# Key projections moved from ahead of the batch loop into its first steps, with bulk loads issued by ScalarE, in a decoder-layer kernel

## The reference, cut to what matters

```python
qkv = jnp.einsum('bsd,de->bse', x, qkv_weights).reshape(-1, 3 * D)      # D = 256, H = 16 heads of Dh = 16
q, k, v = the three thirds of qkv, each reshaped to (-1, S, H, Dh) and transposed to heads
a = q @ k / 4, masked to the lower triangle;  a = softmax(a);  heads = a @ v
x = layernorm(x + heads)
x = layernorm(x + retention-like cross attention of x with ctx, using Wq, Wk, Wv)
x = layernorm(x + shared SwiGLU + top 2 of 8 routed SwiGLU experts)
```

## Time and profile before

| what | value |
|---|---|
| median of 3 executions | 768.1 us (765.79 to 771.39) |
| the profiled execution | 769.79 us |
| its span, first to last instruction | 768.0 us |
| mean granted TensorE clock | 0.971 of 2.4 GHz |
| busy over the span: PE / DVE / ACT / POOL | 92% / 62% / 53% / 43% |

### The profile page before, as it was taken

How to read it: one execution, slowest core, us unless ns; L and a number is a source line. 1 busy time by engine, 2 the same in 40 slices (tenths; PEclk the granted TensorE clock), 3 DMA queues, 4 the chain that set the end, 5 groups by cost and what they waited for, 6 DMA issues and landing times.

```text
span 768.0 us, 19404 instructions
## 1 busy us (share of the span) xinstructions
PE 702.7 (92%) x5464; PEld 531.7 (69%) x5465; DVE 479.0 (62%) x1536; ACT 409.2 (53%) x1167; POOL 333.8 (43%) x483
## 2 busy tenths in 40 slices
PE   6977899999999999999987649999999999999993
PEld 5866788888888888888875315566666666665453
DVE  3555577888888888888865433444444444438984
ACT  0268688888888888888851102333333333312232
POOL 1002233345555555555565553555555555541111
PEclk9999999999999999999999768999999999999998
DMA  8745562223333332333371543322222222218962
GB/s 296 249 146 155 149 220 75 82 65 101 102 90 90 101 112 77 102 101 98 91 235 53 155 138 117 125 89 83 89 82 89 82 89 82 89 59 319 307 213 82
DMA packets 77032, 97.54 MB, mean 127 GB/s; under 512 B 12320, under 2 KB 63264, under 8 KB 75936
## 3 DMA queue, kind: packets, MB, share of 16 engines
q1 hardware_dynamic: 59920, 68.21, 28.5%
q0 software_dynamic: 6816, 19.00, 6.9%
q10 hardware_dynamic: 10224, 9.42, 4.6%
HBM read 60.02 MB, written 36.56 MB: 126 GB/s over the span
## 4 chain that ended last, share of the span: by engine, by line
PE 69%; issue 13%; DVE 4%; POOL 4%; SPq 4%; DMA 4%; ACT 1%; DVEq 0%; POOLq 0%; ACTq 0%
PE ps L996 16%; PE ps L1007 8%; PE ps L783 6%; PE ps L861 4%; PE ps L771 4%; PE ps L793 4%; PE ps L748 4%; PE ps L864 3%; PE ps L885 3%; PE ps L751 3%; DVE products L1269 3%; PE ps L982 2%; POOL sent L640 2%; PE ps L989 2%; PE ps L922 2%
## 5 line engine op out<-in xcount | busy, mean ns | idle before, releaser
L1085 ACT ACTIVATE prob<-ps,nmax 128x128 f32<-128x128 f32 x512 | 146.4, 377 | 29.1 <-DVE nmax L1259 29.0
L996 PE MATMUL ps<-first_use,xgT 128*128 x284 | 135.6, 600 | 1.5 <-ACT xgT L1190 1.5
L1489 DVE TENSOR_TENSOR hid<-ps,attn_only 128x512 f32<-128x512 f32 x71 | 49.1, 692 | 95.6 <-PE ps L996 94.4
L1190 ACT COPY xgT<-ps 128x256 f32<-128x256 f32 x71 | 26.4, 372 | 137.2 <-PE ps L982 137.2
L1259 DVE TENSOR_REDUCE nmax<-ps 128x4 f32<-128x512 f32 x128 | 82.2, 685 | 19.9 <-PE ps L771 18.5
L677 POOL TENSOR_TENSOR gate_h<-hid,sil 128x256 f32<-128x256 f32 x71 | 50.8, 715 | 96.6 <-DVE result_row L1502 83.0
L1092 ACT COPY pT<-ps 128x512 f32<-128x512 f32 x128 | 76.7, 599 | 18.9 <-PE ps L783 14.7
L783 PE MATMUL ps<-tf,prob 128*128 128x128 f32 x512 | 78.2, 275 | 5.7 <-ACT pT L1092 5.7
L996 PEld LDWEIGHTS ps<-first_use,xgT 128*128 128x128 f32 x284 | 54.3, 192 | 40.5 <-issue 37.0
L640 POOL DMA_INDIRECT sent<-packets,pos x64 | 63.7, 995 | 37.3 <-PE ps L771 22.8
L680 POOL DMA_INDIRECT back<-yg,result_row x71 | 71.5, 1007 | 14.3 <-issue 12.4
(11 more groups left out here) (135 smaller groups left out, 1408.8 us busy)
## 6 DMA issues: line engine op xcount, KB each, us to landing
xg<-sent ACTq DMA_DIRECT2D x68, 129.5 KB, 2.1
first_use<-back SPq DMA_DIRECT2D x8, 1024.0 KB, 7.9
k_dram<-first_use SPq DMA_DIRECT2D x4, 1024.0 KB, 4.4
attn_only<-in_x_turned SPq DMA_DIRECT2D x32, 128.0 KB, 3.0
attn_only<-k_dram SPq DMA_DIRECT2D x256, 16.0 KB
attn_only<-in_x SPq DMA_DIRECT2D x32, 128.0 KB, 2.8
attn_only<-in_ctx SPq DMA_DIRECT2D x32, 128.0 KB, 2.9
first_use<-in_L_ffn_rw SPq DMA_DIRECT2D x8, 512.0 KB, 5.2
```

The lines of the kernel that those rows point to most:

```text
L996: mm = eng.matmul(ps[:, r, :], xgT[:, r, c, :], rw1_sb[:, bass.ds(e * (DC * 2 * FFN) + c * 2 * FFN, 2 * FFN)], start=(c == 0), stop=(c == ...
L1085: ins = eng.activation(prob[:, t % 2, 4 * u + n, :], SCORE[u][:, n * P:(n + 1) * P], ACT.Exp, bias=nmax[:, t % 2, 4 * u + n:4 * u + n + 1])
```

## The change

- Keys: a table `K_BANK` gives each of the 16 quarters its PSUM bank. Quarters 0 to 3 (group 0) run ahead of the loop, 4 to 6 at the head of step 0, ahead of its scores; 7 to 9 in the rest of step 0, 10 to 13 in step 1, 14 and 15 in step 2. DVE's copies are spread to match.
- SP no longer loads groups 1 to 3 nor runs `load_small`. ACT issues them: group 1 ahead of its steps once group 0's last piece is in, group 2 at the head of its step 0, group 3 after the first exponentials of step 0, and `load_small` (8 transfers) between the third and the fourth set of exponentials of step 0. The mask table is loaded early on SP with a semaphore of its own.
- The store of group 0 is split: the rows of batch 0 (128 KB), then the rest. SP's stores of groups 1 to 3 move to the ends of its steps 0, 1 and 2.
- Waits for the tables, cross-attention weights and small weights move to steps 3 and 5; the expert weights begin loading in step 4 in place of 3; POOL's clearing of `sent` moves from step 2 to 4.

```diff
+K_BANK = (4, 5, 6, 7, 4, 5, 7, 4, 5, 7, 5, 7, 5, 7, 6, 7)
@@ SP
-            for g in range(1, NG):
-                eng.dma_start(xTu[g][:, :, :, :, :].rearrange("p u c b i -> p (u c b i)"),
-                              x_blocks[g].rearrange("p u n -> p (u n)")).then_inc(xTu_in[g], 16)
-            eng.dma_start(ident, table_f32[:, 0:P]).then_inc(ident_in, 16)
             for n in (0, 2):
                 eng.dma_start(wqkv_sb[:, :, n * D:(n + 1) * D], wqkv_rows[:, :, n * D:(n + 1) * D]).then_inc(w_in, 16)
+            eng.dma_start(xT[:, 0, :, :], x_turned[0]).then_inc(xT_in[0], 16)
+            eng.dma_start(tb[:, :], table_bf16).then_inc(mask_in, 16)
+            eng.dma_start(xT[:, 1, :, :], x_turned[1]).then_inc(xT_in[1], 16)
+            eng.dma_start(ident, table_f32[:, 0:P]).then_inc(ident_in, 16)
...
             def store_k(g):
                 eng.wait_ge(kk_set, g * 4 + 4)
-                eng.dma_start(k_dram[g * GB:(g + 1) * GB].rearrange("b i g f -> (b i) (g f)"),
-                              kk_of(g)).then_inc(k_stored[min(g, 1)], 16)
-
-            load_small()
+                rows = k_dram[g * GB:(g + 1) * GB].rearrange("b i g f -> (b i) (g f)")
+                if g == 0:
+                    eng.dma_start(rows[0:DH, :], kk_of(g)[0:DH, :]).then_inc(k_stored[0], 16)
+                    eng.dma_start(rows[DH:P, :], kk_of(g)[DH:P, :]).then_inc(k_stored[1], 16)
+                else:
+                    eng.dma_start(rows, kk_of(g)).then_inc(k_stored[2], 16)
+
             store_k(0)
@@ SP step
-                    if t == 0:
-                        eng.wait_ge(k_stored[0], 16)
+                    if t < 2:
+                        eng.wait_ge(k_stored[t], 16)
...
-                if n in (-1, 0, 1):
-                    store_k(n + 2)
-                if n == 3:
-                    eng.wait_ge(k_stored[1], 16 * (NG - 1))
-                if 2 < n <= 2 + NE // 2:
+                if n == 4:
+                    eng.wait_ge(k_stored[2], 16 * (NG - 1))
+                if 3 < n <= 3 + NE // 2:
...
                     eng.dma_start(xn[:, t % 2, :], x[t]).then_inc(xn_in[t % 2], 16)
+                if n in (0, 1, 2):
+                    store_k(n + 1)
@@ POOL step
-                if n == 2:
+                if n == 4:
                     eng.wait_ge(zeros_set, 1)
@@ PE
+            def project_ks(first, end):
+
+                for i in range(first, end):
+                    if i == 0:
+                        eng.wait_ge(wk_in, 16)
+                    if i < 4:
+                        eng.wait_ge(first_in[i], 16)
+                    elif i % 4 == 0:
+                        eng.wait_ge(xTu_in[i // 4], 16)
+                    if K_BANK[i] in K_BANK[:i]:
+                        eng.wait_ge(kk_set, i - K_BANK[:i][::-1].index(K_BANK[i]))
+                    project_k(i // 4, i % 4, K_BANK[i])
+
+            project_ks(0, 4)
             eng.wait_ge(w_in, 32)
-            eng.wait_ge(kk_set, 4 * NG - 5)
-            eng.wait_ge(tables_in, 32)
-            eng.wait_ge(xw_in, 48)
-            eng.wait_ge(small_in, 64)
+            eng.wait_ge(mask_in, 16)
             eng.wait_ge(consts_set, 2)
+            eng.wait_ge(kk_set, 3)
@@ PE step
+                if n == 0:
+                    project_ks(4, 7)
                 if n == 1:
-                    eng.wait_ge(kk_set, 13)
+                    eng.wait_ge(ident_in, 16)
+                    eng.wait_ge(kk_set, 8)
...
                 if n == 2:
-                    eng.wait_ge(kk_set, 4 * NG)
+                    eng.wait_ge(kk_set, 13)
...
                 if live(n):
                     scores(n)
                 if n == 0:
-                    eng.wait_ge(kk_set, 9)
-                    project_k(NG - 1, 0, 4)
+                    project_ks(7, 9)
                 if n == 1:
-                    eng.wait_ge(kk_set, 14)
-                    project_k(NG - 1, 3, 5)
+                    project_ks(10, 11)
+                if n == 2:
+                    eng.wait_ge(q_set, 3)
+                    eng.wait_ge(v_set, 3)
+                    project_ks(14, 15)
...
                 if live(n - 1):
                     turn_probs(n - 1, 1)
+                if n == 1:
+                    project_ks(11, 12)
...
                 if live(n - 1):
                     turn_probs(n - 1, 2)
+                if n == 1:
+                    project_ks(12, 13)
+                if n == 2:
+                    project_ks(15, 16)
...
+                if n == 2:
+                    eng.wait_ge(kk_set, 15)
                 if live(n + 1):
                     project(n + 1)
                 if n == 0:
-                    eng.wait_ge(kk_set, 12)
-                    project_k(NG - 1, 1, 5)
-                    project_k(NG - 1, 2, 7)
+                    project_ks(9, 10)
+                if n == 1:
+                    project_ks(13, 14)
@@ ACT
+            def load_small():
+                eng.dma_start(tf[:, P:], table_f32[:, P:]).then_inc(tables_in, 16)
+                for w, src in ((xwq_sb, xwq), (xwk_sb, xwk), (xwv_sb, xwv)):
+                    eng.dma_start(w[:, :, :], src.rearrange("(c p) n -> p c n", p=P)).then_inc(xw_in, 16)
+                eng.dma_start(gate_w_sb[:, :, :], gate_w.rearrange("(c p) n -> p c n", p=P)).then_inc(small_in, 16)
+                eng.dma_start(gate_b_sb[:, 0:NE], gate_b.rearrange("(o n) -> o n", o=1).broadcast_to([P, NE])).then_inc(small_in, 16)
+                eng.dma_start(sb1_sb[:, :], sb1[0].rearrange("(c p) -> p c", p=P), allow_slow_non_contiguous=True).then_inc(small_in, 16)
+                eng.dma_start(sb2_sb[:, :], sb2.broadcast_to([P, D])).then_inc(small_in, 16)
+
+            eng.wait_ge(first_in[3], 16)
+            load_blocks(1)
@@ ACT step
+                if n == 0:
+                    load_blocks(2)
...
                 if live(n):
                     exps(n, 1)
+                if n == 0:
+                    load_blocks(3)
...
                 if live(n):
                     exps(n, 3)
+                if n == 0:
+                    load_small()
@@ DVE step
+                if n == 0:
+                    out_ks(4, 7)
...
+                if n == 1:
+                    out_ks(9, 10)
+                if n == 2:
+                    out_ks(13, 14)
...
                 if n == 0:
-                    for j, bank in enumerate((4, 5, 7)):
-                        out_k(NG - 1, j, bank)
+                    out_ks(7, 9)
                 if n == 1:
-                    out_k(NG - 1, 3, 5)
+                    out_ks(10, 12)
+                if n == 2:
+                    out_ks(14, 15)
...
+                if n == 2:
+                    out_ks(15, 16)
...
                 if live(n) and live(n + 1):
                     lay_mask(n + 1, 3)
+                if n == 1:
+                    out_ks(12, 13)
```

More of the change, by code:

```diff
@@ L292, in decoder_kernel @@
         kk_set = sem("kk_set")
-        k_stored = [sem("k_stored_first"), sem("k_stored_rest")]
+        k_stored = [sem("k_stored_batch"), sem("k_stored_group"), sem("k_stored_rest")]
+        mask_in = sem("mask_in")
         xT_in = [sem("xT_in0"), sem("xT_in1")]
@@ L467, in step @@
                 t = n + 2
-                if live(t):
+                if live(t) and t > 1:
                     after(eng, qv_made, t - 1)
@@ L835, in step @@
             def step(n):
+                if n == 0:
+                    project_ks(4, 7)
                 if n == 1:
-                    eng.wait_ge(kk_set, 13)
+                    eng.wait_ge(ident_in, 16)
+                    eng.wait_ge(kk_set, 8)
+                if n == 3:
+                    eng.wait_ge(tables_in, 16)
+                    eng.wait_ge(xw_in, 48)
+                if n == 5:
+                    eng.wait_ge(small_in, 64)
                 if live(n - 1):
@@ L957, in step @@
                     eng.wait_ge(x1_set, t + 1)
+                    if n == 2:
+                        eng.wait_ge(kk_set, 4 * NG)
                     after(eng, gc_set, n - 4)
@@ L1241, in _, with out_ks @@
         def _(eng):
-            def out_k(g, j, bank):
-                eng.wait_ge(k_made, g * 4 + j + 1)
-                eng.tensor_copy(kk_of(g).rearrange("p (a u) -> p u a", u=NU)[:, 2 * j:2 * j + 2, :],
-                                ps[:, bank, :].rearrange("p (u a) -> p u a", u=2)).then_inc(kk_set, 1)
-            for g in range(NG - 1):
-                for j in range(4):
-                    out_k(g, j, 4 + j)
-            eng.wait_ge(tables_in, 32)
-            eng.wait_ge(consts_set, 2)
-            eng.tensor_copy(base[:, :], region_rows).then_inc(base_set, 1)
-            eng.tensor_copy(zeros[:, D:PACKET], padding_end).then_inc(zeros_set, 1)
+            def out_ks(first, end):
+                for i in range(first, end):
+                    eng.wait_ge(k_made, i + 1)
+                    eng.tensor_copy(kk_of(i // 4).rearrange("p (a u) -> p u a", u=NU)[:, i % 4 * 2:i % 4 * 2 + 2, :],
```

(8 more changed lines are left out.)

28 lines of the change are left out of this document (7 added, 21 removed).

## The result

The changed kernel takes 778.1 us (median of 6, 773.7 to 781.2) against 768.8 us (median of 6) for the kernel before: ratio 1.010, 95% interval 1.006 to 1.014. The forecast was 767.5 us, no change within 1%, with 760.0 to 774.5 as range. It is slower, and outside the range.

A forecast was written before the change was run, and what follows sets the result against it. Taken as bound ahead of the loop: PE's quarters and SP's chain of waits, ending together near 32 us. Terms -8.5 + 2.55 + 3.65 + 2.1 - 0.3 = -0.5 us; from median 768.1, 767.6, rounded to 767.5; range 760 to 774.5.

The forecast's parts named there:

- the prediction's own signs of being wrong: Small-load issues summing to under 3.5 or over 8 us, or step 3's scores over 3 us off 64.4.
- Scores of batch 0: End of the work ahead of the loop: scores start at 24.0 us, 8.5 us ahead of before; at worst 25.3.
- Step 0: First loop step, ended by ACT's chain: 13.4 us in place of 10.85.
- L: Time of ACT's eight small-load issues in step 0: taken as 5.0 us, ends 2.8 and 11.4.
- 8.4 + L: Length of step 0: ACT's exponentials, masks, queries and group 3's issue, 8.4 us, plus the small-load issues.
- Step 1: Four key quarters in place of one, PE filling the step: 14.8 us with half-clock loss, ends 13.1 and 16.5.
- step 2: Two key quarters in place of none, one hidden in PE's wait: 12.2 us, 2.1 more; ends 10.3 and 13.6.
- The wait for the context: PE's 2.6 us wait in step 4 moves to step 5 with the expert weights: -0.3 us.
- POOL's clearing (0.9 MB) runs ahead of the expert weights: nothing: Clearing of sent, moved to step 4 ahead of the expert weights, was priced at no cost.
- The tail: From step 31's scores to the end: no change, 0 us.
- C: Rival, slower: step 0's small-load issues held on ACT as on SP, 11.4 us, costing 6.4; 774 us; chance 0.15.
- D: Rival: transfers interleave, first scores at 25.3 us and quarter 12's input late; 768.9 us; chance 0.12.

The follow-up runs named there:

- e1: Changed kernel with ACT issuing group 2's inputs right behind group 1's: ratio 1.006 to the kernel before; scores of batch 0 at 24.69 us.
- e2: Changed kernel with the eight small loads issued by POOL instead of ACT: ratio 0.999 to the kernel before; step 0 11.21 us, step 1 12.73 us.
- e7: Changed kernel with group 2's inputs early, small loads issued by POOL and clearing in step 8: 765.0 us against 769.6 for the kernel before, ratio 0.992.
- e9: Kernel before with SP issuing the context ahead of the expert weights: ratio 1.000 to the kernel before.
- e13: As e7, but with the key quarters where the kernel before had them, 12 ahead of the loop: ratio 1.002 to the kernel before.
- e3: Changed kernel with POOL's clearing in step 8 instead of 4: one execution, context wait 2.45 us in place of 3.70, step 5 15.29 in place of 17.61.
- e11: Changed kernel with the small loads reordered, four little ones first, tables last: one execution, issues sum to 5.3 us, step 0 11.66 us.
- e5: Changed kernel with sb1 and sb2 exchanged in the small loads, sb1 last: one execution, issues sum to 7.5 us.
- e6: Changed kernel with ACT issuing groups 1 to 3 and the small loads ahead of its steps: one execution, scores of batch 0 at 29.60 us.
- e10: Changed kernel with SP issuing groups 1 to 3 and the small loads ahead of group 0's store, ACT none: ratio 1.003 to the kernel before.
- e12: As e7, but group 0's keys are stored in one transfer instead of two: one execution, scores of batch 0 at 26.02 us.

## Why the prediction was wrong, point by point

The forecast of the profiled execution was -0.5 us and the measured span +8.4. Of the 8.9 between them, 4.0 stand in the late keys, 1.8 in step 0, 2.5 in the wait for the context and 1.3 behind the loop; steps 1 and 2 came out 0.9 better. Both of the prediction's own signs of being wrong were met: the issues sum to 8.8 us (over 8), and step 3's scores start at 69.39, 5.0 us off 64.4.

**Scores of batch 0: 24.0 forecast, 28.05 measured.** The step "At worst another 4.4 us, 25.3 us. I take 24.0" failed. The store's landing was right (18.9). Wrong was that the loads of 16 KB behind it would take the 4.9 us of the earlier trace rows: beside group 2's megabyte, issued by ACT at 16.4 and not at 18.0, it was 9.0 us, and without it (e1) 5.3, with the scores at 24.69. Interleaving was named in the prediction, and I gave that rival 0.12 and 1.3 us; it was worth 3.4. The bound was an addition of times at full rate for the large transfers alone; the eight small loads behind them were issued more slowly too, in 5.3 us where the earlier trace rows had 3.6.

**Step 0: L = 5.0 forecast, 8.8 measured.** The term "I take 8 x 0.47 = 3.8 and 1.2 for those that had been slow: L = 5.0" failed. The mechanism was right (ACT held by its own issues, e2) and its size wrong, toward the end at 11.4 that SP's rows had given. What I had argued from, that less was queued than in the earlier trace rows, didn't hold: six issues took 0.33 to 0.53 us each, as I assumed, and the last two 1.13 and 4.68. The term 8.4 + L was itself too large by 2.1, since ACT issues before its earlier exponentials have ended; the two errors hid each other in part.

**Step 1: +3.65 forecast, +3.19 measured; step 2: +2.1, +1.70.** Step 1 is right, by the steps given: PE fills step 1 at 14.34 us with a stretch at half clock, and without it (e2, e7) it is 12.73, near the 13.1 of the sum. Step 2 is 11.8 in every variant with two quarters in it, at full clock with PE busy 10.34 of 11.83, which is the mechanism that was argued. But it is 11.8 as well without a quarter in e9 and e13, at a clock of 0.86. Against an execution like those the two quarters cost nothing; that the difference came out near 2.1 rests on the one profile before that had 10.13, and is partly luck.

**The wait for the context: -0.3 forecast, +2.2 measured.** It moved to step 5, as said. "POOL's clearing (0.9 MB) runs ahead of the expert weights: nothing" is the step that failed: 2.3 us by the pair with e3.

**The tail: 0 forecast, +1.3 measured.** A stretch at half clock fell on matmuls; not explained, and within what this part scatters between executions.

Of the rivals, C (held issues) and D (interleaving) both came true in kind, together and with the clearing, where I had given each alone a chance and a sum on its own. Neither has its size: C had L at 11.4 (measured 8.8), D the first scores at 25.3 (measured 28.05). Two of the three causes were named; that all three err to the same side wasn't reckoned with.

## What to carry to other kernels

Moving work out of a prologue pays only when everything that ends there is moved: here PE's quarters and SP's queue ended together, and either alone gained nothing. Don't put bulk loads into the middle of an engine that computes: an issue can be held for several us, and then all behind it on that engine. POOL, which had nothing to do in these steps, issued them without holding anyone (e2, e7); where they have to stay, their order matters (e11, one execution). Transfers with a deadline (here the keys coming back, and the context) go ahead of bulk that has none, and bulk on another queue still runs in their way (e1). And a baseline of one profile can hold a step that is 1.7 us shorter than in the next execution: compare more than one before a small term counts as confirmed.

## What the runs showed of the hardware that I had not expected

- An issue on ACT's queue was held when several transfers stood in it: 4.68 us at the eighth small load, 3.68 at the seventh (e5), 4.08 at the seventh and 1.88 at the eighth (e1), 7.95 with two more megabytes ahead (e6), 1.79 when the tables came last (e11). SP's queue does it too: 4.00 and 3.54 us (e10). POOL's took 0.56 to 0.79 each for the same eight. On ACT, with the tables first, the hold ended within 1.7 us of the tables' landing, in e5 and e6 shortly ahead of it. What is counted, bytes, rows or transfers, stays open.
- ACT issued the tables at 32.21 us while exponentials written ahead of that issue ran until 34.72: with no semaphore between them, the issue didn't wait for the engine's earlier computing.
- A wait of PE can be paid twice: 5.67 us of waiting for keys were followed by scores at 2.09 us instead of 1.17 and a quarter at 3.46 instead of 1.89; after waits of 1.87, 1.96 and 2.39 us (e1, e7, e12) both ran at full clock. The length of the wait alone doesn't decide: behind 2.12 us ahead of step 1 the kernel before had its quarter at 3.44 us, and half clock came in e9's and e13's step 2 and not in the same step before.
